# A hybrid recurrence, sparse-layer and attention block: the order of work inside a tile of the sparse layers

## What is computed

```python
x = x + recurrent_block(layernorm(x))
x = x + sparse_layer(layernorm(x))
x = x + attention(layernorm(x))
x = x + sparse_layer(layernorm(x))
```

```python
score_out = softmax(_gated_bottleneck(x2d, so_...))      # 256 logits a row
s_v_out, s_i_out = top_k(score_out, 32)
full = x @ weight
out_branch = scatter(take(full, s_i_out) * s_v_out)
score_in = softmax(_gated_bottleneck(x2d, si_...))
s_v_in, s_i_in = top_k(score_in, 32)
x_sparse = scatter(take(x, s_i_in) * s_v_in)
return out_branch + x_sparse @ weight + bias
```

## Time and profile before

| | us |
|---|---|
| median of 3 runs (1374.25 to 1379.99) | 1378.51 |
| the profiled execution | 1377.57 |
| its span, first to last instruction | 1375.6 |
| first sparse layer, from 277 to 500 | 223 |
| attention, from 500 to 1156 | 656 |
| second sparse layer, from 1156 to 1376 | 220 |

### The profile page before, as it was taken

The page is one execution under the profiler, slowest core; times in us unless marked ns, Lnnn a source line. Parts: engine busy times, 40 slices in busy tenths (PEclk is TensorE's granted clock), DMA queues, the critical chain, the costliest instruction groups (busy, mean ns, idle before and its releaser), DMA issues.

```text
span 1375.6 us, 30660 instructions
## 1 busy us (share of the span) xinstructions
PE 1219.7 (89%) x10192; PEld 745.8 (54%) x10192; DVE 1145.5 (83%) x3141; ACT 1054.7 (77%) x2351; POOL 962.1 (70%) x1100
## 2 busy tenths in 40 slices
PE   3999999867888879999999999999999999677776
PEld 1455555434455536665666666666666667344443
DVE  6999998589998888888777787877878754799998
ACT  3332333677899869999999989999999995787776
POOL 4456644368777777778777778777777773388887
PEclk9899999989999999999999999999999999799998
DMA  6200000000012000010000000000000000000000
GB/s 174 77 1 1 0 0 1 1 1 1 10 38 78 27 21 25 25 26 25 25 14 14 2 2 2 2 3 2 2 2 2 2 3 1 1 31 16 25 22 32
DMA packets 35529, 25.32 MB, mean 18 GB/s; under 512 B 16358, under 2 KB 32044, under 8 KB 35372
## 3 DMA queue, kind: packets, MB, share of 16 engines
q1 hardware_dynamic: 35372, 23.36, 6.0%
HBM read 14.89 MB, written 8.39 MB: 17 GB/s over the span
## 4 chain that ended last, share of the span: by engine, by line
PE 58%; ACT 13%; issue 12%; DVE 11%; POOL 4%; DVEq 0%; DMA 0%; SPq 0%; POOLq 0%; ACTq 0%
PE banks L2023 7%; PE banks L2025 6%; PE banks L2011 6%; DVE arena L1535 4%; PE banks L1761 4%; PE banks L1969 4%; PE banks L1720 4%; PE banks L2040 4%; PE banks L2041 4%; PE banks L2042 3%; ACT arena L1174 3%; DVE arena L1530 3%; ACT arena L1182 2%; PE banks L1748 2%; PE banks L1776 2%
## 5 line engine op out<-in xcount | busy, mean ns | idle before, releaser
L839 POOL TENSOR_TENSOR arena<-arena 128x512 f16<-128x512 f32 x383 | 437.6, 1161 | 150.5 <-ACT arena L1182 146.6
L1174 ACT ACTIVATE arena<-banks 128x512 f32<-128x512 f32 x512 | 302.9, 599 | 45.5 <-PE banks L2025 40.8
L1611 DVE TENSOR_REDUCE arena<-banks 128x1 f32<-128x512 f32 x512 | 325.8, 680 | 4.0 <-PE banks L2011 1.8
L1182 ACT ACTIVATE arena<-arena 128x512 f16<-128x512 f32 x512 | 316.2, 632 | 0.0
L1530 DVE MAX8 arena<-arena 128x8 f32<-128x256 f32 x512 | 190.4, 414 | 27.4 <-issue 15.9
L2040 PE MATMUL banks<-arena 128*128 128x65 f16 x2016 | 211.4, 193 | 0.9
L2041 PE MATMUL banks<-arena 128*128 128x64 f16 x2016 | 211.5, 195 | 0.0
L2042 PE MATMUL banks<-arena 128*128 128x65 f16 x2016 | 210.6, 193 | 0.0
L1637 DVE TENSOR_TENSOR arena<-arena 128x512 f16<-128x512 f32 x129 | 107.0, 829 | 123.2 <-ACT arena L1182 123.0
L1535 DVE MATCH_REPLACE8 arena<-arena 128x256 f32<-128x256 f32 x512 | 206.2, 411 | 0.9 <-issue 0.2
L2040 PEld LDWEIGHTS banks<-arena 128*128 128x128 f16 x2016 | 187.9, 96 | 31.8 <-issue 9.9
(11 more groups left out here) (229 smaller groups left out, 2545.1 us busy)
## 6 DMA issues: line engine op xcount, KB each, us to landing
arena<-q_store SPq DMA_DIRECT2D x48, 128.0 KB, 2.7
x<-in_L_attn_a_x SPq DMA_DIRECT2D x8, 512.0 KB, 3.9
q_store<-arena SPq DMA_DIRECT2D x32, 128.0 KB, 1.8
out<-x SPq DMA_DIRECT2D x7, 512.0 KB, 2.9
arena<-arena SPq DMA_DIRECT2D x64, 1.0 KB, 1.9
arena<-in_L_attn_a_W_in SPq DMA_DIRECT2D x1, 768.0 KB, 5.8
arena<-in_L_attn_a_W_mid SPq DMA_DIRECT2D x1, 512.0 KB, 7.6
arena<-in_L_attn_a_w_w SPq DMA_DIRECT2D x2, 256.0 KB, 8.0
```

Source lines behind the costliest of these rows:

```text
L839: nc.gpsimd.tensor_tensor(pr_lo[c][:, kt, :], pr[:, kt, :], pr_hi[c][:, kt, :], ALU.subtract).then_inc(a_lP, 1)
L1174: nc.scalar.activation(pr[:, kt, :], ps[6 + kt % 2][:, :], ACT.Exp, scale=SM_SCALE).then_inc(a_P, 1)
L1182: nc.scalar.activation(pr_hi[c][:, kt, :], pr[:, kt, :], ACT.Copy).then_inc(a_hi, 1)
L1611: nc.vector.tensor_reduce(mx_half[c][:, i // 2, i % 2:i % 2 + 1], ps[n % MAX_BANKS][:, :], X, ALU.max).then_inc(a_mx, 1)
```

## The change

The change touches the sparse layers and the head work in the first.

- `lg` has three buffers. TensorE computes the logits of tile t + 3 in tile t, not those of t + 2, and ScalarE copies them then. The logits of three tiles are copied between pieces of the Gelu.
- On TensorE the turned input of tile t comes ahead of the logits of t + 3, and the product of the turned input behind them. This holds in both sparse layers.
- `head_first` and `head_second` do on both engines what `HEAD_AT` lists for t in tile t. The first piece listed stands ahead of the turned input on TensorE and of its copy on ScalarE, the others behind the logits. The low part stands at the end of the tile.
- The sixteen normed rows are written by GpSimd at the end of its tail, each one tile earlier than ScalarE wrote them. Their place in GpSimd's list is behind the reciprocal roots.
- The eight score products at the end of the first layer stand behind the turned input of tile 31, and not ahead of it.

```diff
-        lg = [carve([2, D]) for _ in range(2)]
+        lg = [carve([2, D]) for _ in range(LG_RING)]
...
-        HEAD_ROWS_AT = {8: (0, 1), 9: (2, 3), 12: (4,), 13: (5,), 14: (6, 7), 16: (8,), 17: (9,), 18: (10,), 19: (11,),
-                        21: (12,), 22: (13,), 23: (14,), 24: (15,)}
+        HEAD_ROWS_AT = {7: (0, 1), 8: (2, 3), 11: (4,), 12: (5,), 13: (6, 7), 15: (8,), 16: (9,), 17: (10,), 18: (11,),
+                        20: (12,), 21: (13,), 22: (14,), 23: (15,)}
...
+                    if f == 0:
+                        head_rows(t)
+
+            def head_rows(t):
+
+                for r in HEAD_ROWS_AT.get(t, ()):
+                    k, j = r // TPC, r % TPC
+                    if j == 0:
+                        pool.wait_ge(n_p, 4 * group_of["ffn", k] + 4)
+                        pool.wait_ge(s_tps, 2 * (LN_ATTN + max(0, k - 1)) if k != 1 else 2 * LN_ATTN)
+                    last = nc.gpsimd.tensor_scalar(z_rows[k % 2][:, j, :], x[:, r, :], rs[:, r, 0:1], rs[:, r, 1:2],
+                                                   ALU.mult, ALU.add)
+                    if j == TPC - 1:
+                        last.then_inc(s_z, 1)
...
-                    if n in (1, 3):
-                        ffn_logits(f, n // 2, n // 2)
+                    if n in (1, 3, 5):
+                        ffn_logits(f, n // 2, 0)
...
                     ffn_rest(f, t, q)
-                    if f == 0:
-                        head_first(t)
                     ffn_zT(f, t + 2, q)
                     ffn_exp(f, t + 1, 1 - q)
+                    if f == 0:
+                        head_first(t, slice(0, 1))
                     ffn_sT(f, t, q)
                     ffn_fs(f, t, q)
-                    ffn_logits(f, t + 2, q)
+                    if t + 3 < NT:
+                        ffn_logits(f, t + 3, 1 - q)
+                    if f == 0:
+                        head_first(t, slice(1, None))
+                    ffn_gs(f, t, q)
                     if f == 0:
                         head_second(t)
-                    ffn_gs(f, t, q)
...
                 for t in range(NT):
                     ffn_full(f, t, t % 2)
+                    if t == 0:
+                        ffn_logits(f, 2, 0)
                     if t + 2 < NT:
-                        ffn_front(f, t + 2, t % 2)
+                        ffn_z_turned(f, t + 2, t % 2)
+                    if f == 0:
+                        head_first(t, slice(0, 1))
+                    ffn_in_turned(f, t, t % 2)
+                    if t + 3 < NT:
+                        ffn_logits(f, t + 3, 1 - t % 2)
+                    if f == 0 and t == NT - 1:
+                        first_maxima()
+                    if f == 0:
+                        head_first(t, slice(1, None))
+                    ffn_in(f, t, t % 2)
                     if f == 0:
                         head_second(t)
-                    ffn_in(f, t, t % 2)
-                    if f == 0:
-                        head_first(t)
```

More of the change, by code:

```diff
@@ L42 @@
 AHEAD = 2
+LG_RING = 3
 B_IN, P_LOG, B_MID, W1B, W2B = 0, 6, 12, 16, 18
@@ L1035, in ffn_exp @@
                 for i in range(2):
-                    nc.scalar.activation(ex[p][:, i, :], lg[p][:, i, :], ACT.Exp, bias=nm[p][:, i:i + 1],
+                    nc.scalar.activation(ex[p][:, i, :], lg[t % LG_RING][:, i, :], ACT.Exp, bias=nm[p][:, i:i + 1],
                                          accum_out=sm[p][:, i:i + 1]).then_inc(f_e, 1)
@@ L1182, in high, with head_first @@
                 nc.scalar.activation(pr_hi[c][:, kt, :], pr[:, kt, :], ACT.Copy).then_inc(a_hi, 1)
-            def head_first(t):
-                for what, k, part, bank in HEAD_AT.get(t - 1, ()):
+            def head_first(t, which):
+                for what, k, part, bank in HEAD_AT.get(t, ())[which]:
                     B, c = k // 2, k % 2
@@ L1205, in head_second @@
             def head_second(t):
-                for what, k, part, bank in HEAD_AT.get(t - 1, ()):
+                for what, k, part, bank in HEAD_AT.get(t, ()):
                     B, c = k // 2, k % 2
@@ L1880, in ffn_full, with ffn_in_turned @@
                 last.then_inc(f_fps, 1)
+            def ffn_in_turned(f, t, p):
+                pe.wait_ge(f_s, t + f * NT + 1)
+                for k in range(KB2):
+                    last = nc.tensor.transpose(ps[4][:, k * P:k * P + P], sx[p][:, k * P:k * P + P], ident[:, :])
+                last.then_inc(f_sps, 1)
             def ffn_in(f, t, p):
@@ L1885, in ffn_in @@
                 pe.wait_ge(f_gs, T + CREDIT["f_gs"])
-                pe.wait_ge(f_s, T + 1)
-                for k in range(KB2):
-                    last = nc.tensor.transpose(ps[4][:, k * P:k * P + P], sx[p][:, k * P:k * P + P], ident[:, :])
-                last.then_inc(f_sps, 1)
                 pe.wait_ge(f_sT, T + 1)
@@ L2060, in _, with head_first @@
             WEIGHTED_AT = {3: 0, 4: 1, 6: 2, 7: 3}
-            def head_first(t):
-                for what, k, part, bank in HEAD_AT.get(t, ()):
+            def head_first(t, which):
+                for what, k, part, bank in HEAD_AT.get(t, ())[which]:
                     B, c = k // 2, k % 2
@@ L2099, in head_second, with first_maxima @@
                            start=False, stop=True, skip_group_check=True).then_inc(h_qmps, 1)
-                if t == NT - 1:
-                    pe.wait_ge(f_lg, NT)
-                    for i in range(2):
-                        max_scores(0, i)
-                    pe.wait_ge(*head_read[2])
-                    for i in range(2, HALVES):
-                        max_scores(0, i)
+            def first_maxima():
+                pe.wait_ge(f_lg, NT)
+                for i in range(2):
+                    max_scores(0, i)
+                pe.wait_ge(*head_read[2])
+                for i in range(2, HALVES):
+                    max_scores(0, i)
             ffn(0)
```

11 lines of the change are left out of this document (3 added, 8 removed).

## The result

The changed kernel takes **1396.44 us** (median, 1396.27 to 1396.95), the kernel before 1377.57 (1374.25 to 1379.99): a ratio of 1.0139, with a 95% interval of 1.0117 to 1.0162. So it is slower by 1.4%, and the forecast of 1394 us lies 2.4 us under it. The execution profiled after took 1396.95 us for a span of 1395.2.

The account below looks back on a forecast made before the run. VectorE was taken to bound light tiles (5.8 us), TensorE those with head work. Second layer 12.5 us longer plus first layer 3.0 gives 15.5, added to the 1378.51 median: 1394 us, range 1373 to 1407.

Parts of the forecast that it names:

- the ring: Sparse-layer tiles: loop from second exponentials through GpSimd's products, turned input and its product to the next exponentials; 5.3 us before.
- Part 3: First layer: tile 11 3.5 us later, including two clock falls at 2.4; tiles 11 to 29 3.5 us earlier.
- Part 1: TensorE order, both layers: logits join the light ring, 5.66 us; second layer gets 11 clock falls at 1.2 us each.
- The idle piece: TensorE's wait before the turned input, said to grow by the logits' 1.09 us to about 1.8 to 2.0.
- Part 2: Logits three tiles ahead: second layer's tile 1 exponentials start 3.2 us later; with ring and falls, that layer 12.5 us longer.
- 0.2, 2.2 and 0.4 against 3.7: First layer to tile 11: light ring 0.2, GpSimd rows 2.2, first and second turns 0.4, against 3.7 from VectorE statistics.
- a ring of 6.15 us: First layer's loaded tiles with a query: 5.66 plus 0.49 for the low part's copy, against 6.39 before; 4.3 won.
- The hand-over: First layer's end to attention: first maximum 3.1 us later behind tile 31's turned input, 0.5 returned; first layer 3.0 longer.
- (a): Rival: clock falls stay beside the ring or don't grow in number; 1378.5 us, no change; chance 0.24 with (d).
- (b): Rival: VectorE's waits in loaded tiles go, if their ring is under 5.9 us and clock holds; 1369.5 us, chance 0.11.
- (d): Rival: turned input waits for GpSimd's product, not TensorE, so the piece in front hides nothing; alone gives (a), together 0.24.
- (c): Rival: GpSimd rows block VectorE in the first layer, 8.8 us on top of (a); 1387.3 us, chance 0.07.

Follow-up runs that it names:

- e1: Changed kernel with the logits ahead of the turned input again in the second layer alone: 1383.05 us.
- e2: Changed kernel plus one idle TensorE product ahead of the turned input, in the second layer and tiles 0 to 8 of the first: 1375.60 us.
- e3: Changed kernel with the sixteen normalised rows back on ScalarE: 1402.62 us.
- e9: Kernel before with only the sixteen normalised rows moved to GpSimd, one tile earlier: 1379.43 us.
- e5: Kernel before plus one idle product ahead of the turned input, in the second layer and tiles 0 to 8 of the first: 1380.62 us.
- e10: Changed kernel plus idle products (second layer, first layer's tiles 0 to 9, 29 to 31) and first maxima ahead of tile 31's turned input: 1373.25 us.
- e12: e10 plus idle products in TensorE's waits of both Gelu stretches: 1371.09 us.
- e7: Changed kernel with only the first maxima's two score products moved ahead of tile 31's turned input: 1397.03 us.

## Why the prediction was right, point by point

**The mechanism** held: slower, through falls of the clock that came to lie on the ring. e1 (13.4 us back with the old order) and e2 (20.8 us back with the clock kept up) show it from two sides, and most of the signs that the prediction named were seen: clock 0.83 (under 0.85), fifteen falls, fourteen of them with L1883 inside, VectorE idle 15.6 us (over 8), the first maximum 8.0 us behind the end of the search (over 3). The start of the second layer was 2.06 us late instead of about 3, and of the loaded tiles with one query and no statistics, for which 6.1 to 6.2 us were said, four run at 6.00 to 6.10 and two at 6.33 and 6.53 (Part 3).

**Part 1, sizes.** The light ring was forecast at 5.66 us and is 5.51: turn and logits 1.36 (1.30 said), product to the next L1058 1.93 (2.03 said), turned input behind GpSimd's product 0.78 (0.87 said). The idle piece was to be 1.8 to 2.0 us and is 1.63. Falls: 11 said, 15 seen. Price: 1.2 said over a ring of 5.66; worked out, it is (186.70 - 30 x 5.50) / 15 = 1.45 each over a ring of 5.50. Against e2, which has the same order and no falls (172.18), it is 14.5 / 15 = 0.97 each, because VectorE's pace and not the ring is the floor there. The errors, a ring too long and falls too few and too cheap, cancel in part, and that is luck: 183.0 us were forecast for the thirty tiles, 186.70 came.

**Part 2.** The start was to be 3.2 us late and is 2.06 (18.21 against 16.15). The second layer in all: 12.5 said, 15.0 measured.

**Part 3.** Tile 11 was to be 3.5 late; measured from the start of the search it is 86.68 against 78.62, 8.1. The start is 2.5 late (2.0 said), and tiles 1 to 11 take 5.5 us more. The term that failed is "two falls: 2.4": there were five behind the start, and in e2, which has none there, the same tiles take 6.2 us less than in the changed kernel. So the price of 1.2 a fall was right there and the number was wrong. The other terms from tile 1 on (0.2, 2.2 and 0.4 against 3.7) say 0.9 earlier in all, and e2 shows 0.7 earlier.

Loaded tiles: 3.5 earlier said, 4.6 seen. The forecast took a ring of 6.15 us and 0.8 for the extra pieces. A ring of 5.50 and the 0.49 for the low part's copy give 5.99; from one product on GpSimd to the next, tiles 12, 21, 23 and 28, with one query each, take 6.05, 6.10, 6.06 and 6.00 us, tiles 13 and 17, which also carry one query, 6.53 and 6.33, and tile 18, with statistics besides, 7.59. So the ring was put about 0.1 us too long for the fastest of them; how much of the 0.8 was paid no run shows. e3 and e9 add what the sum did not have: most of this gain needs the rows and the rest of the change together.

**The hand-over.** First maximum 1.57 us behind the product of tile 31 said, 1.93 seen; 3.1 us late said, 5.4 seen, as the tiles ahead of it were late too and the clock low. First layer in all, from the start of the search to the second layer: 3.0 said, 5.9 measured (904.05 against 898.18), less the 1.6 us by which this execution started its search earlier. So 15.0 + 5.9 - 1.6 = 19.3 is the 19.4 us between the two profiled executions, against a forecast of 15.5. The total came closer than its parts by luck: the two layers were 5.4 us longer than said, of which 1.6 was hidden by the early start of the search. The forecast also stood on a median of 1378.51, 0.9 above the later one, so 2.4 us of error in the time is 3.4 in the difference (18.9 measured, 15.5 said).

**The rivals.** (a), falls beside the ring: refuted in the changed kernel, and true of the kernel before, where VectorE is as busy with the falls as e5's is without. Its sum has a slip: without the 2.4 and the 0.4 for falls the first layer is 0.2 longer, not 0.6, which makes 1378.0. Nor would five falls instead of eleven have brought the forecast inside 6.9 us of no change, as the chances assume: 15.5 - 7.2 is 8.3. (b), the gain wins: this is what remains when the clock is kept up and the maxima are moved, e10 and e12, 1373.3 and 1371.1 us where (b) said 1369.5, though the loaded ring did not come under the 5.9 us that it asked for. (d) held: the turned input of every tile from 12 to 28 starts 0.78 us behind GpSimd's product, with the query in front of it. (c), rows block VectorE: refuted by e3 and by the trace. In the changed kernel the eleven MAX8 that overlap a row on GpSimd (L839) average 414 ns and the twenty MATCH_REPLACE8 409, all others 413 and 409; before it was 414 and 411 over the whole kernel. The Trainium skill ("SBUF — State Buffer", section "SBUF: two separate sides") has one of the two engines block on a shared pair of ports when VectorE's instruction is in a 2-port mode, or reads two SBUF inputs while GpSimd's reads SBUF. No run here shows that rule at work; the rows of both search instructions show one input of 128x256.

```profile
L1546 DVE MAX8 arena<-arena 128x8 f32<-128x256 f32 x512 | 190.2, 413 | 34.5 <-ACT arena L1058 23.2
...
L1551 DVE MATCH_REPLACE8 arena<-arena 128x256 f32<-128x256 f32 x512 | 205.8, 409 | 0.9 <-issue 0.2
```

## What to carry to other kernels

Moving TensorE's work out of a wait leaves a larger idle piece there, and here the granted clock fell more often with it: look at what stands directly behind the idle piece, since in fourteen of fifteen falls that ran at half speed, at least in part. When the slack on a ring (here 0.3 us a tile) is smaller than the price of a fall (1.45), try the idle product before you give up the order, and put it only where TensorE has a wait to fill; e5 shows in tile 0 what it does elsewhere. It told in one run that the order was sound, and turned a loss of 1.4% into a gain of 0.3 to 0.5% together with the maxima moved ahead. And parts of a change can need each other: in the loaded tiles the rows on GpSimd were worth 3.8 us in the new order and 1.7 in the old, where tiles 0 to 11 lost more than that.

## What was not expected of the hardware

Idle pieces of TensorE of only 1.63 us, one in each tile of 5.5 us, went with fifteen falls of the granted clock to 0.50 (1.2 GHz) in thirty tiles. So it took no long pause to lose the clock here, and one product of 1.02 us a tile (L1939) kept it.

What decides about a fall these runs don't show. The length of the piece ahead of the turned input is not enough: in e2 it is 0.78 us in ten tiles and 1.09 in most others, with no fall, while the kernel before has mostly 1.2 us there, another 0.47 ahead of the product, and eight falls. The idle product both shortens the piece and adds work, and no run parts the two.

How many falls a stretch gets differs between runs with the same code there (from tile 1 to tile 31 of the second layer fifteen in the changed kernel, 57 us at the low clock; sixteen in e7, 61 us), and the stretch differs with them by 2.5 us. An edit worth less than that can't be priced in a kernel whose ring pays for the falls; keep the clock up first, then compare.
